# High halves of the stacked loads asked for by GpSimd, low ones by SyncE, and two expert-weight loads and a table build placed later

## The reference

```
x = layernorm(x + proj(softmax(l2norm(q) l2norm(k)^T / sqrt(8) / temperature) v) + b)   # q, k, v from x
x = layernorm(x + softmax(causal((q2 k2^T + skew(q2 Er^T)) / sqrt(8))) v2)              # q2 from x; k2, v2 from ctx
e = argmax(softmax(x router_w + router_b));  h = x w1[e] + b1[e];  a, g = split(h)
x = layernorm(x + (a * sigmoid(g)) w2[e] + b2[e])                                       # 8 experts, top 1
```

## Time and profile before

| | us |
|---|---|
| three runs | 289.67 median, 287.71 to 290.94 |
| profiled execution, its own time | 290.45 |
| span of its trace | 288.7 |
| PE busy in the span | 235.4 |
| DVE busy | 202.0 |
| ACT busy | 140.7 |
| POOL busy | 91.8 |

### The profile page before, as it was taken

One profiled execution on the slowest core, in us unless ns is written; L12 is line 12 of the kernel. 1 busy time (PEld: TensorE's weight loads), 2 busy tenths in 40 slices (PEclk: granted clock), 3 DMA queues, 4 the chain that ended last, 5 costly groups with the idle time before them and its releaser, 6 DMA issues.

```text
span 288.7 us, 8043 instructions
## 1 busy us (share of the span) xinstructions
PE 235.4 (82%) x3170; PEld 173.4 (60%) x3171; DVE 202.0 (70%) x579; ACT 140.7 (49%) x326; POOL 91.8 (32%) x128
## 2 busy tenths in 40 slices
...
GB/s 65 195 396 184 41 168 154 109 76 179 218 60 166 104 119 22 94 189 213 94 111 112 3 41 70 190 115 115 194 175 61 16 20 187 187 179 345 141 7 0
DMA packets 30036, 36.92 MB, mean 128 GB/s; under 512 B 6967, under 2 KB 23333, under 8 KB 29616
## 3 DMA queue, kind: packets, MB, share of 16 engines
...
q10 hardware_dynamic: 256, 0.03, 0.1%
...
## 4 chain that ended last, share of the span: by engine, by line
PE 33%; issue 20%; DVE 17%; POOL 10%; DMA 9%; ACT 7%; SPq 2%; POOLq 1%; DVEq 0%; ACTq 0%
DVE negm L1084 6%; POOL out L777 5%; PE SB L1529 4%; PE MA L1365 3%; DMA w_sb<-parts_a 3%; POOL rs L772 3%; PE SA L1409 3%; DMA shift_a<-nmT 2%; DMA parts_a<-SpA 2%; PE MB L1345 2%; PE SA L1424 2%; PE SB L1388 2%; PE MA L1435 2%; ACT P L851 2%; SPq L467 2%
## 5 line engine op out<-in xcount | busy, mean ns | idle before, releaser
L1084 DVE TENSOR_REDUCE negm<-SA 128x2 bf16<-128x512 f32 x64 | 41.2, 685 | 11.4 <-PE SA L1409 11.0
L851 ACT ACTIVATE P<-SA 128x512 f32<-128x512 f32 x64 | 35.7, 599 | 14.6 <-PE SA L1424 13.1
L1163 DVE TENSOR_REDUCE negm<-MB 128x4 bf16<-128x512 bf16 x32 | 22.0, 686 | 8.3 <-PE MB L1345 8.0
L735 POOL TENSOR_TENSOR rs<-ve,half 128x2 f32<-128x2 f32 (+1 forms) x9 | 6.1, 682 | 64.9 <-DVE ve L1045 64.9
L797 ACT ACTIVATE Sb<-SB 128x512 bf16<-128x512 f32 x22 | 13.1, 597 | 24.5 <-PE SB L1529 24.2
L889 ACT ACTIVATE P2b<-SB 128x1024 f32<-128x1024 f32 x14 | 14.1, 1023 | 8.9 <-PE SB L1548 8.8
L1409 PE MATMUL SA<-w_sb 96*128 96x256 bf16 x64 | 12.5, 297 | 6.7 <-DVE negm L1084 4.7
L1524 PE MATMUL SB<-QH,KZ 128*128 128x64 bf16 x320 | 16.9, 198 | 1.1 <-DMA QH<-parts_b 1.1
L1435 PE MATMUL MA<-P,V 128*32 128x256 f32 x256 | 17.3, 402 | 0.0
L1548 PE MATMUL SB<-identb,negm 128*128 128x128 bf16 x176 | 14.3, 219 | 3.0 <-issue 1.9
L777 POOL DMA_INDIRECT out<-P,token x15 | 15.3, 1019 | 3.8 <-issue 3.1
...
## 6 DMA issues: line engine op xcount, KB each, us to landing
...
w_sb<-in_w POOLq DMA_DIRECT2D x8, 512.0 KB, 5.1
...
w_sb<-parts_a SPq DMA_DIRECT2D x8, 192.0 KB, 3.9
parts_b<-SpB SPq DMA_DIRECT2D x8, 192.0 KB, 2.1
KZ<-parts_b SPq DMA_DIRECT2D x8, 192.0 KB, 3.3
...
P2b<-in_w SPq DMA_DIRECT2D x3, 512.0 KB, 5.3
```

Source lines behind the costliest of these rows:

```text
L851: a.activation(P1[:, grp % 2, kt, 2 * i:2 * i + 2, :].rearrange("p h t -> p (h t)"), SA[:, bank_a("st", b, u), :], ACT.Exp).then_inc(s["ex ...
L1084: v.tensor_reduce(out=negm1[:, hp // 4, qt, :, hp % 4], in_=SA[:, bank_a("d", b, u), :].rearrange("p (g k) -> p g k", g=2), axis=AX.X, op= ...
L1163: v.tensor_reduce(out=negm2[:, qb, :], in_=MBb[:, 0:512].rearrange("p (c k) -> p c k", c=4), axis=AX.X, op=ALU.max, negate=True).then_inc( ...
```

## The change

In both attentions the two high loads go from SP to POOL (`high_stacks` at the step `A1.qsin.b`, `high_queries` at a new step `A2.zin.b`), with semaphores of their own (`qs_high`, `qz_high`, `qh_high`), and everyone who waited for four loads waits for two and two. `A1.qsin.1` moves ahead of `A1.k0.1`. `A2.zin.b` stands after `A1.qkn.2` (b = 0), `A1.qkn.3` (b = 1), `A2.q2T.2` and `A2.q2T.3`. `W.u3` moves behind `A2.ln1.2`, `W.pk0` behind `A2.zin.2` and `W.u4` behind `B.sc1.2`. The pace of these three becomes: `A1.d2.3` for u3, the landing of the low Z of batch 2 for pk0, `B.sc1.2` for u4.

```diff
-    A2.st4.0 A2.st5.0 A1.k6.0 A1.k0.1 A2.st6.0 A2.st7.0 A1.qsin.1 A2.pv0.0 ...
+    A2.st4.0 A2.st5.0 A1.k6.0 A1.qsin.1 A1.k0.1 A2.st6.0 A2.st7.0 A2.pv0.0 ...
...
-    A2.st11.2 A2.st12.2 B.tr3.1 W.u3.0 A2.k2T.2 W.pk0.0 A2.st13.2 B.sh2.1 W.u4.0 A2.st14.2 ...
+    B.sc4.1 A1.qsin.3 A2.st11.2 A2.st12.2 B.tr3.1 A2.k2T.2 A2.st13.2 B.sh2.1 A2.st14.2 ...
+    ... A2.proj.2 A2.ln1.2 W.u3.0 B.sc6.1 B.sh5.1 ... A2.q2T.2 A2.zin.2 W.pk0.0 A1.d5.3 ...
+    ... B.sc0.2 B.sc1.2 W.u4.0 B.tr0.2 ...
+    ... A2.nm1.3 ... A2.q2T.3 A2.zin.3 B.v.3 B.gt0.3 B.sc0.3 B.ln2.2 ...
@@ q_k_in
-                for g in range(2):
-                    rows = slice(g * SR, (g + 1) * SR)
-                    load(QSs[b % 2][rows, :, :]..., "qs_in")
-                    load(KSs[b % 2][rows, :, :], half_stack(parts_a, 1, g), "qs_in")
+                load(*query_rows(b, 0), "qs_in")
+                load(*key_rows(b, 0), "qs_in")
@@ cross_queries
-                for half_ in (0, 64):
-                    load(Zs[b % 2][half_:half_ + SR, :, q], stack(parts_b, 0)[:, :, q], "qz_in")
+                load(*cross_rows(b, 0), "qz_in")
...
-                by_half(lambda at, heads: QHs[b % 2][at:at + SR, heads, q], parts_b, 0, q, "qh_in")
+                load(*cross_half(b, 0), "qh_in")
@@ new on POOL
+            def high_stacks(b):
+                wait(pool, "st_full", (b - 1) * 16)
+                pool.wait_ge(s["pa_out"], b * 96)
+                for rows, parts in (query_rows(b, 1), key_rows(b, 1)):
+                    pool.dma_start(rows, parts).then_inc(s["qs_high"], 16)
+
+            def high_queries(b):
+                wait(pool, "sc_full", (b - 1) * NQB)
+                if b < 2:
+                    pool.wait_ge(s["z_fill" if b == 0 else "qz_fill"], 1)
+                    pool.wait_ge(s["kz_fill" if b == 0 else "qh_fill"], 1)
+                pool.wait_ge(s["pq_out"], b * 48 + 48)
+                for name, (rows, parts) in (("qz_high", cross_rows(b, 1)), ("qh_high", cross_half(b, 1))):
+                    pool.dma_start(rows, parts).then_inc(s[name], 16)
```

More of the change, by code:

```diff
@@ L70 @@
     A1.qkv.2 A1.shT0.1 A1.shin0.1 A2.x1T.0 A1.d8.1 A1.d9.1 A1.d10.1 A1.d11.1 A2.q2T.0 A1.d12.1 A1.d13.1 A1.d14.1
[L71 to L94, removed]
+    A1.d15.1 A1.qkn.2 A2.zin.0 A2.st0.1 A2.st1.1 A1.shT1.1 A1.qkT.2 A1.shin1.1 B.build.0 A2.st2.1 A2.st3.1 A2.st4.1
@@ new lines @@
+    A2.st5.1 A2.st6.1 A2.st7.1 B.rest.0 A2.pv0.1 A2.pv1.1 A2.st8.1 A2.cx.1 B.sc0.0 A2.nm0.1 A2.st9.1 A2.st10.1
+    B.tr0.0 B.sc1.0 A2.st11.1 A2.st12.1 B.sc2.0 A1.qsin.2 B.tr1.0 A2.xpb.1 A2.st13.1 A2.st14.1 A2.k2T.1 A2.st15.1
+    B.sc3.0 B.tr2.0 B.sh0.0 A2.pv2.1 A2.pv3.1 B.sh1.0 A1.d0.2 B.tr3.0 A1.d1.2 W.u1.0 W.v7.0 A2.nm1.1 A1.d2.2 B.sc4.0
+    B.sh2.0 A2.oT.1 B.sh3.0 A1.d3.2 B.tr4.0 A2.proj.1 A2.ln1.1 B.sc5.0 B.pv0.0 A1.d4.2 A2.x1T.1 A1.d5.2 B.sh4.0
+    B.nm0.0 A2.q2T.1 A1.d6.2 A1.d7.2 B.tr5.0 A1.vcp.2 A1.qkv.3 B.sc6.0 B.sh5.0 A1.d8.2 A1.d9.2 B.tr6.0 A1.qkn.3
@@ new lines @@
+    A2.zin.1 B.sc7.0 A1.d10.2 B.sh6.0 A1.shT0.2 A1.shin0.2 B.tr7.0 A1.d11.2 A1.d12.2 A2.xpb.2 B.sh7.0 A1.d13.2
+    A1.d14.2 B.build.1 B.pv1.0 A1.d15.2 A2.st0.2 B.nm1.0 A2.st1.2 A2.st2.2 B.ln2.0 B.v.1 A2.st3.2 W.u2.0 A1.shT1.2
+    A1.shin1.2 B.sc0.1 B.rest.1 A2.st4.2 A2.st5.2 A2.pv0.2 A2.st6.2 B.x2T.0 A2.st7.2 B.sc1.1 A2.cx.2 B.lg.0 A2.pv1.2
+    B.tr0.1 B.sc2.1 B.tr1.1 A2.st8.2 A2.st9.2 B.sh0.1 B.rk.0 A1.qkT.3 B.sh1.1 B.sc3.1 B.tr2.1 A2.nm0.2 A2.st10.2
+    B.sc4.1 A1.qsin.3 A2.st11.2 A2.st12.2 B.tr3.1 A2.k2T.2 A2.st13.2 B.sh2.1 A2.st14.2 B.sh3.1 A2.st15.2 B.tr4.1
@@ new lines @@
+    A2.pv2.2 B.sc5.1 A2.pv3.2 B.sh4.1 B.tr5.1 A2.nm1.2 A1.d0.3 A1.d1.3 A2.oT.2 A1.d2.3 A2.proj.2 A2.ln1.2 W.u3.0
+    B.sc6.1 B.sh5.1 B.pv0.1 A1.d3.3 A1.d4.3 A2.x1T.2 B.nm0.1 A2.q2T.2 A2.zin.2 W.pk0.0 A1.d5.3 B.tr6.1 A1.d6.3
+    A1.vcp.3 B.sc7.1 A1.d7.3 B.tr7.1 A1.d8.3 B.sh6.1 A1.d9.3 B.sh7.1 A1.d10.3 A1.shT0.3 A1.shin0.3 A1.d11.3 A1.d12.3
+    B.pv1.1 A1.d13.3 A1.d14.3 B.v.2 B.build.2 B.nm1.1 B.rest.2 A1.d15.3 B.sc0.2 B.sc1.2 W.u4.0 B.tr0.2 A2.st0.3
+    B.sc2.2 A2.st1.3 B.tr1.2 A2.st2.3 B.sc3.2 B.tr2.2 B.sh0.2 B.sh1.2 B.ln2.1 A2.st3.3 B.tr3.2 A1.shT1.3 A1.shin1.3
@@ new lines @@
+    A2.st4.3 B.sc4.2 A2.st5.3 A2.pv0.3 B.x2T.1 A2.st6.3 A2.st7.3 B.lg.1 B.sh2.2 B.sh3.2 B.tr4.2 A2.st8.3 A2.st9.3
+    A2.xpb.3 A2.pv1.3 B.rk.1 B.sc5.2 A2.st10.3 B.pv0.2 A2.cx.3 A2.nm0.3 B.sh4.2 B.tr5.2 A2.k2T.3 A2.st11.3 A2.st12.3
+    B.sh5.2 B.sc6.2 A2.st13.3 A2.st14.3 A2.pv2.3 A2.st15.3 W.v0.0 B.tr6.2 B.sc7.2 W.v1.0 A2.pv3.3 B.nm0.2 B.sh6.2
+    A2.nm1.3 B.tr7.2 A2.oT.3 B.sh7.2 A2.proj.3 B.pv1.2 A2.ln1.3 W.v2.0 A2.x1T.3 B.nm1.2 A2.q2T.3 A2.zin.3 B.v.3
+    B.gt0.3 B.sc0.3 B.ln2.2 B.gt1.3 B.tr0.3 W.u6.0 B.sc1.3 B.x2T.2 B.lg.2 B.tr1.3 B.sc2.3 B.tr2.3 B.sh0.3 B.sh1.3
@@ L453, in build, with stack, half_stack, query_rows @@
         XG_GROUPS = (("xg_in0", 0, 1), ("xg_in1", 1, 3), ("xg_in2", 3, E), ("xg_in3", E, NTILE))
+        def stack(parts, which):
+            return parts[which].rearrange("w (d h) t -> (w d) h t", h=H)
+        def half_stack(parts, which, g):
+            return parts[which].rearrange("w (d g j) t -> g (w d) j t", g=2, j=H // 2)[g]
+        def query_rows(b, g):
+            return (QSs[b % 2][g * SR:(g + 1) * SR, :, :].rearrange("r (a g j) t -> r g a (j t)", g=2, a=2)[:, g, :, :],
+                    half_stack(parts_a, 0, g).rearrange("r (a j) t -> r a (j t)", a=2))
+        def key_rows(b, g):
+            return KSs[b % 2][g * SR:(g + 1) * SR, :, :], half_stack(parts_a, 1, g)
+        def cross_rows(b, half_):
+            q = OTHERS if b == NB - 1 else slice(0, NT)
+            return Zs[b % 2][64 * half_:64 * half_ + SR, :, q], stack(parts_b, 0)[:, :, q]
+        def cross_half(b, half_):
+            q = OTHERS if b == NB - 1 else slice(0, NT)
+            heads = slice(half_ * H // 2, (half_ + 1) * H // 2)
+            return QHs[b % 2][64 * half_:64 * half_ + SR, heads, q], stack(parts_b, 0)[:, heads, q]
         def group_of(j):
@@ L492, in write_parts @@
                     load(dst[which, at:at + n].rearrange("w p t -> p w t"), src, name)
[L494 to L499, removed]
             def next_x(b):
```

37 lines of the change are left out of this document (21 added, 16 removed).

## The result

The changed kernel takes **295.91 us** (median of 4 runs, 293.82 to 298.35) against 290.31 (4 runs, 287.71 to 291.47) of the kernel before on the same chip: ratio **1.0183**, 95% interval 1.0121 to 1.0245. It is slower, and above the range of 284.9 to 292.3. The profiled execution took 295.16 us, its span 293.1, 4.4 us more than before.

A forecast was written before the change was run, and what follows sets the result against it. It took PE and DVE, alternating at nearly every batch step, as the bound, so only their visible waits count. Terms summed to -0.8 us: 289.65 against the profiled 290.45, median 288.9 us, range 284.9 to 292.3.

The forecast's parts named there:

- Query loads: Cross-attention loads of Z and QH, batches 0 and 2: two queues serve them in nearly the same order, -0.3 us each.
- a rival with a chance of 0.10: Z complete later if POOL's Z load comes behind SP's QH; only W.u3's move remains, 290.2 us; chance 0.10.
- Root of ln2.2: Router's root on POOL, batch 3: two high query loads issued ahead of it delay it, +1.2 us.
- The rival of a slow description: POOL's issue of 256 B pieces at 4 ns each holds up the router: +4.5 us, total 292.2 us; chance 0.13.
- Stacks of batch 3: With W.u3 gone, the last parts_a write takes 2.8 us and PE starts at the stacks earlier: -2.0 us.
- W.pk0: Its copies at the new place fall on DVE's second parity multiply of batch 2 and slow it: +1.0 us.
- W.u3: Behind the root at 140.60 it meets the three parts_b writes of batch 2: +0.3 us.
- W.u4: Moved to about 162 us, where no stack moves: 0.
- Clock: PE's matmuls at 1.2 GHz after waits, as behind batch 3's stacks, partly regain full clock: -0.7 us.
- The side-by-side rival: SP's and POOL's queues run side by side, so the load waits go whole: 284.9 us; chance 0.25.

The follow-up runs named there:

- e12: The changed kernel itself, unaltered, run again on another chip beside the kernel before: 1.0247 of before, median 295.67 us.
- e7: Kernel before with the three weight steps later and SP alone asking for Z low, QH low, Z high, QH high: 1.0171 of before.
- e9: Kernel before with only the three weight steps (W.u3, W.pk0, W.u4) moved later, all loads on SP: 0.9984 of before.
- e5: Changed kernel with the self-attention's high loads, and batch 3's cross-attention high loads, back on SP: 1.0122 of before.
- e11: Kernel before with only W.pk0 moved behind A2.q2T.2: 1.0133 of before.
- e3: Changed kernel with the cross-attention's high loads back on SP in their old order, the self-attention's still on POOL: 0.9894 of before.

## Why the prediction was wrong

The forecast's sum was -0.8 us; the span grew by 4.4. Term by term:

- **Query loads, -0.3 and -0.3: the step that failed.** "POOL's high loads arrive at about the time at which SP's high ones did. So I expect the engines to work through the same 1152 KB in nearly the same order." The first half held (Z high starts 0.50 us after Z low, 0.36 before) and so did the total (9.25 against 8.98 us); the order did not. I didn't see that QH low moves up on SP's queue when Z high leaves it, to 0.36 us after Z low, and so ahead of a POOL load that starts 0.5 us behind SP. Measured: +1.3 in batch 0 instead of -0.3; in batch 2 1.6 of idle time in e12, and none in the profiled run, where DVE was late for another reason. e7 shows the order to be the cause. The mechanism was written down as half of a rival with a chance of 0.10 ("Z is complete later than before"), but priced with W.u3 alone and never against DVE's wait for Z, 0.82 us before, which was no row of mine. A transfer that already ends an idle time has no cover.
- **Root of ln2.2, +1.2: right**, 1.96 instead of 0.83 us, +1.13 (1.5 in e12 against e9). Its parts were off: the two DMAs take 0.78 and 0.66 us, not 2.3 together, and the missing part is POOL's start 0.54 us behind SP's. e5 removes it. The rival of a slow description (4 ns for each piece) is out.
- **Stacks of batch 3, -2.0.** The write fell to 2.15 us and the four operations to 1.55, both as forecast, but the wait only from 1.67 to 1.37. POOL's request comes 0.52 us behind SP's, and from the first request to the matmul it is 6.10 us, 5.34 before. In the five kernels with high stacks on POOL it is 5.70 to 6.45, 5.96 on average, in the others 5.25 to 5.71, 5.44 on average (e11's 6.08 left out), so about 0.5 us. DVE is 1.6 us late at 128.04 (126.41 before) and PE's matmul only 0.3 (136.55 and 136.27), so the term is -1.4.
- **W.pk0, +1.0.** The first multiply took 1.09 instead of 0.69, the second 1.75 as before, where I wrote over 2.5. There the copies gave way: 5.97 us for six instead of 4.38. Term +0.4, and it belongs to the copies: e3, with all of Z on SP in the old order and no wait, has it too, with 1.31 us for the first multiply. One reading of mine was wrong: the first of the four operations of the earlier trace rows ran beside W.pk0's clearing (126.82 to 129.50), not beside its copies.
- **W.u3, +0.3, and W.u4, 0.** W.u3 lands at 144.76 and the first `parts_b` write of batch 2 goes out at 144.87: nothing. W.u4 has no wait beside it either.
- **Clock, -0.7: not measurable in the total.** At the stacks of batch 3, where it was forecast, the clock did come back: 1.00 in 138 to 139 us instead of 0.50, and DVE, 0.3 us late at their matmul, was 0.3 early at 143 us. But the granted clock of single runs of one program goes from 0.903 to 0.960 (e9), more than any edit moves it. In the profiled execution it cost 1.9 us further on: at 156.63 DVE waits 3.36 us for PE, which ran at the lower clock of 0.50 (the window below); in e12, the same kernel, that wait is 1.50, as before.
- **The tail, no term at all:** +1.14.

1.3 + 0.4 + 1.1 - 1.4 + 1.9 + 1.1 = 4.4 us, the growth of the span. That it comes out so well is partly luck: the sum leaves out the 0.6 us that DVE gained behind the stacks, and between these two profiled runs DVE had made up the delay of batch 0 by 110.8 us and was late again at 111.9, by 0.9 us, so this pair alone doesn't show that the 1.3 reached the end. e12 against e9 is the better evidence. The window of the clock, before and then in the changed kernel, with columns as in the earlier trace rows:

```profile
153.00:154.00 1.00, 1.00 (x41) 0.80 (x33) 0.00 (x0) 0.00 (x0) 0.00 (x0) 1.00 1.15 184
```

```profile
153.00:154.00 1.00, 1.00 (x28) 0.92 (x24) 0.27 (x1) 0.00 (x0) 0.53 (x1) 0.50 1.01 188
```

The side-by-side rival (0.25) is dead: 9.25 us for four loads on two queues. The Trainium skill says so in one line (DMA: Bandwidth & Descriptors, Rules for kernel authors: spreading DMAs over SP, ACT and GpSimd doesn't help bandwidth, they use the same 16 engines, and only issue time is saved). The trace agrees, and adds that the spreading has prices of its own: the later start, the order, and the tail. I had used the neighbouring rule for the size of the term, and read "no gain" as "no cost".
